# Causal mask of the transposed scores by selection on GpSimd, K stacks on ScalarE's queue, gap rows written by SyncE

## What is computed

```python
h = _layernorm(x) * (1 + ca) + sa
q = h @ w_dq.T @ w_uq.T ; kv = h @ w_dkv.T @ w_ukv.T ; k, v = split(kv)
attn = einsum('bhqd,bhkd->bhqk', q, k) * SCALE + triu(-inf, k=1)   # causal
x = x + ga * (softmax(attn) @ v) @ w_out.T
h = _layernorm(x) * (1 + cb) + sb
top = argmax(softmax(h @ Wg.T))              # expert 0 (gelu) or 1 (relu)
x = x + gb * where(top == 0, expert0(h), expert1(h))
```

## Time and profile before

| What | Value |
|---|---|
| runs before, median (lowest, highest) | 584.45 us (584.08, 586.81) |
| profiled execution, whole | 587.29 us |
| its span | 585.5 us |
| PE / DVE / ACT / POOL busy | 80% / 74% / 50% / 39% |
| granted clock of TensorE, mean | 0.901 |

### The profile page before, as it was taken

One profiled execution on the slowest core, in us unless ns is written; L12 is line 12 of the kernel. 1 busy time (PEld: TensorE's weight loads), 2 busy tenths in 40 slices (PEclk: granted clock), 3 DMA queues, 4 the chain that ended last, 5 costly groups with the idle time before them and its releaser, 6 DMA issues. The chain is left out here.

```text
span 585.5 us, 11643 instructions
## 1 busy us (share of the span) xinstructions
PE 466.7 (80%) x4137; PEld 368.5 (63%) x4137; DVE 432.9 (74%) x988; ACT 293.1 (50%) x425; POOL 227.6 (39%) x245
## 2 busy tenths in 40 slices
PE   4634799998978989989989889857705999999950
PEld 4323577776766867767767677634504988888840
DVE  3666576998879878978988798742651699989970
ACT  1342366754635547547447356414402777766630
POOL 8422122334414334334344234273240045455565
PEclk9958799998989889989989899976955999999995
DMA  8578459768748678788688497384339604460111
GB/s 259 181 105 113 80 100 145 99 127 177 101 137 184 103 159 162 129 165 159 127 171 120 110 190 121 98 314 158 119 127 343 231 19 158 150 213 4 37 54 54
DMA packets 58696, 82.02 MB, mean 140 GB/s; under 512 B 7039, under 2 KB 47104, under 8 KB 58640
## 3 DMA queue, kind: packets, MB, share of 16 engines
q1 hardware_dynamic: 52576, 59.37, 48.8%
q0 software_dynamic: 5248, 21.53, 10.9%
q10 hardware_dynamic: 816, 0.39, 0.3%
HBM read 34.12 MB, written 22.11 MB: 96 GB/s over the span
## 5 line engine op out<-in xcount | busy, mean ns | idle before, releaser
L1109 DVE TENSOR_REDUCE mx<-ps_s 128x2 f32<-128x512 f32 (+1 forms) x192 | 124.2, 685 | 49.6 <-PE ps_s L436 47.9
L860 ACT ACTIVATE p_all<-ps_t 128x1024 f32<-128x1024 f32 x93 | 95.3, 1024 | 119.3 <-PE ps_t L436 107.9
L456 PE MATMUL ps_s<-ks,qs 96*128 96x256 bf16 (+1 forms) x512 | 73.6, 253 | 41.1 <-issue 32.8
L456 PEld LDWEIGHTS ps_s<-ks,qs 96*128 96x128 bf16 x512 | 39.6, 100 | 57.5 <-issue 47.2
L482 PE MATMUL ps_t<-qs,ks 99*128 99x128 bf16 (+1 forms) x496 | 61.0, 258 | 6.8 <-DMA qs<-mx_rows 3.1
L436 PE MATMUL ps_s<-future_b,ident_b 128*128 128x256 bf16 (+1 forms) x192 | 62.4, 325 | 0.0
L1360 POOL TENSOR_TENSOR comb<-z,xs 128x512 f32<-128x512 f32 x16 | 20.6, 1285 | 98.3 <-DVE z L1172 98.3
L482 PEld LDWEIGHTS ps_t<-qs,ks 99*128 99x128 bf16 x496 | 38.8, 101 | 21.8 <-issue 12.3
L1467 POOL TENSOR_TENSOR tile_rows<-tile_rows 128x512 f32<-128x512 f32 x18 | 26.3, 1464 | 62.6 <-DVE tile_rows L1292 62.5
L1348 POOL TENSOR_TENSOR ln_rs<-ln_ve,neg_half 128x2 f32<-128x2 f32 x32 | 22.7, 710 | 64.8 <-DVE ln_ve L960 63.7
L403 PE MATMUL ps_s<-down_w,hid_hi 128*128 128x256 f32 x144 | 41.5, 288 | 4.9 <-DVE hid_lo L1272 4.9
(11 more groups left out here) (210 smaller groups left out, 1251.7 us busy)
## 6 DMA issues: line engine op xcount, KB each, us to landing
qs<-parts_q SPq DMA_DIRECT2D x96, 128.0 KB
ks<-parts_k SPq DMA_DIRECT2D x96, 128.0 KB
tile_rows<-sorted_scratch SPq DMA_DIRECT2D x9, 1026.0 KB, 11.7
rows<-mod_rows_scratch SPq DMA_DIRECT2D x16, 384.0 KB, 4.7
tile_rows<-sorted_scratch SPq DMA_DIRECT2D x9, 512.0 KB, 5.3
xs<-x SPq DMA_DIRECT2D x16, 256.0 KB, 5.0
comb<-mod_rows_scratch SPq DMA_DIRECT2D x32, 128.0 KB, 4.4
p_all<-wmod SPq DMA_DIRECT2D x1, 1024.0 KB, 5.9
```

The source lines that it names most:

```text
L456: pe.matmul(ps_s[:, n * width:(n + 1) * width], qs[b.third][0:R, h, tile * P:(tile + 1) * P], ks[b.third][0:R, h, 0:width], start=n % a_ba ...
L860: act.activation((p0, p1)[tile][:, h0:h0 + n, :], scores_t(b, c)[:].rearrange("p (h s) -> p h s", h=n), ACT.Exp, scale=SCALE).then_inc(exp ...
L1109: dve.tensor_reduce(mx[:, tile, h0:h0 + n], ps_s[:, 512 * bank:512 * (bank + 1)].rearrange("p (h k) -> p h k", h=n), AX_X, ALU.max).then_i ...
```

## The change

- The two `past_b` matmuls of every transposed chunk go. In their place `hide_future` on POOL replaces, in `p0` and `p1` after the exponential, what lies above the diagonal by zero, with one `affine_select` per chunk (96 in all: 64 of 128 x 512 elements, 32 of 128 x 1024). `values` waits for `exp_masked` instead of `exp_done`.
- `stack_k` of parts 0 and 1 (five DMAs a batch) moves from SyncE's queue to ScalarE's; part 2 stays on SyncE's. On ACT `k_second` moves ahead of `exponentials(at(3), 0)`; on DVE `k_rest` moves ahead of `place`; on POOL `k_third` and `number_rows` move ahead and `put_rows` moves to the end of the step.
- `fill_gap` with its 12 indirect DMAs goes. After the last batch SyncE reads the gap's first row from `gap_slot` (a copy of `n_first`) and writes exactly 512 rows from `wa` by two plain DMAs, columns 0 to 255 ahead of `load_g(0)`, the others behind it. `load_rest` waits for the second; `load_g` runs three tiles ahead instead of one.
- The set-up on POOL loses one memset, one select and one copy.

```diff
@@ SyncE
                 stack_q(at(1), 0)
                 stack_q(at(1), 1)
-                stack_k(at(1), 0)
                 stack_q(at(1), 2)
-                stack_k(at(1), 1)
-                stack_k(at(1), 2)
+                stack_k3(at(1))
...
+            sp.wait_ge(gap_slot_ready, 1)
+            gap_rows = sorted_dram[bass.ds(sp.value_load(gap_slot[0:1, 0:1], min_val=0, max_val=TOKENS), TS), :].rearrange("(j p) w -> p j w", p=P)
+            some = wa[0][:].rearrange("p k f -> p (k f)").bitcast(F32)
+            sp.dma_start(gap_rows[:, :, 0:D], some[:, 0:D].unsqueeze(1).to_broadcast([P, TJ, D])).then_inc(g_filled, 16)
             for n in range(2):
                 sp.wait_ge(put[n], 16 * NB)
+            sp.wait_ge(g_filled, 16)
             load_g(0)
+            sp.dma_start(gap_rows[:, :, D:ROW], some[:, D:ROW].unsqueeze(1).to_broadcast([P, TJ, ROW - D])).then_inc(rest_filled, 16)
+            load_g(1)
+            load_g(2)
+            sp.wait_ge(rest_filled, 16)
             for i in range(NT):
-                load_g(i + 1)
                 load_rest(i)
+                load_g(i + 3)
@@ TensorE, st_chunk and values
-                for bank in range(2):
-                    mm = masked(dst[:, bank * 512:(bank + 1) * 512], a_bank, 0, past_b)
                 mm.then_inc(st_done, 1)
...
-                pe.wait_ge(exp_done, CH * b.n + ST_OF_GROUP[g])
+                pe.wait_ge(exp_masked, CH * b.n + ST_OF_GROUP[g])
@@ ScalarE
+            def stack_k(b, part):
+                if b.off:
+                    return
+                wait(act, st_done, CH * (b.n - 2))
+                wait_alone(act)
+                act.wait_ge((k1_ready, k2_ready)[part], b.n + 1)
+                for n in range(NSPLIT):
+                    if SPLITS[n][1] == part:
+                        act.dma_start(ks[b.third][n * HD:(n + 1) * HD, :, :], parts_k[:, part, :]).then_inc(k_in[b.pair], 16)
...
                 values_copy(at(4), 1)
+                stack_k(at(1), 0)
+                k_second(at(1))
                 exponentials(at(3), 0)
+                stack_k(at(1), 1)
                 v_copy(at(1))
-                k_second(at(1))
                 exponentials(at(3), 1)
@@ GpSimd
+            def hide_future(b, c):
+                if b.off:
+                    return
+                pool.wait_ge(exp_done, CH * b.n + c + 1)
+                tile, h0, n = ST[c]
+                diag = (p0, p1)[tile][:, h0:h0 + n, 0:P]
+                pool.affine_select(out=diag, in_=diag, compare_op=ALU.is_ge, fill=0.0, base=0,
+                                   pattern=[[0, n], [1, P]], channel_multiplier=-1).then_inc(exp_masked, 1)
```

More of the change, by code:

```diff
@@ L116, in block_kernel @@
         row_of = [sb(f"row_of{i}", [P, TJ], I32) for i in range(2)]
[L117 to L120, removed]
+        gap_slot = sb("gap_slot", [P, 1], I32)
         attention = ctx.enter_context(ExitStack())
@@ L181, in block_kernel @@
         cT_raw, c_silu = mx[:], mx_rest[:]
-        past, future, below = (flat[0][:, 4 * D + i * P:4 * D + (i + 1) * P] for i in range(3))
+        future, below = (flat[0][:, 4 * D + i * P:4 * D + (i + 1) * P] for i in range(2))
         mod_rows = flat[1][0:NB, 0:4 * D].rearrange("p (r d) -> p r d", d=D)
@@ L211, in block_kernel @@
         s_done, max_done, max_split, mt_done = (sem(n) for n in "s_done max_done max_split mt_done".split())
-        mt_ready, st_done, exp_done, pv_done, o_ready = (sem(n) for n in "mt_ready st_done exp_done pv_done o_ready".split())
+        mt_ready, st_done, exp_done, exp_masked, pv_done, o_ready = (sem(n) for n in
+            "mt_ready st_done exp_done exp_masked pv_done o_ready".split())
         ot_done, rden_ready, attn_ready, at_done, a_hi_ready, a_lo_ready, op_done, gated_ready, x1_ready = (sem(n) for n in
@@ L247, in block_kernel @@
         LAGS = 6
-        CONSTS = 13
+        CONSTS = 10
         TABLES = 7
@@ L324, in stack_q, with stack_k3 @@
                 stack(b, part, 0, parts_q, qs, (q1_ready, q2_ready, q3_ready), q_in)
-            def stack_k(b, part):
-                stack(b, part, 1, parts_k, ks, (k1_ready, k2_ready, k3_ready), k_in)
+            def stack_k3(b):
+                stack(b, 2, 1, parts_k, ks, (k1_ready, k2_ready, k3_ready), k_in)
             load_x(Batch(0, NB))
@@ L481, in st_chunk @@
                 for h in range(n):
-                    pe.matmul(dst[:, h * width:(h + 1) * width], ks[b.third][0:RM, h0 + h, tile * P:(tile + 1) * P],
-                              qs[b.third][0:RM, h0 + h, tile * P:S], start=h % a_bank == 0, stop=False)
-                for bank in range(2):
-                    mm = masked(dst[:, bank * 512:(bank + 1) * 512], a_bank, 0, past_b)
+                    mm = pe.matmul(dst[:, h * width:(h + 1) * width], ks[b.third][0:RM, h0 + h, tile * P:(tile + 1) * P],
+                              qs[b.third][0:RM, h0 + h, tile * P:S], start=h % a_bank == 0, stop=h % a_bank == a_bank - 1)
                 mm.then_inc(st_done, 1)
@@ L1198, in step @@
                 row_max(at(2), 2)
+                k_rest(at(1))
                 place(at(6))
[L1200 removed]
                 second_stats(at(5))
@@ L1220, in _ @@
             dve.wait_ge(total_ready, 1)
+            dve.tensor_copy(gap_slot[:], n_first[:]).then_inc(gap_slot_ready, 1)
+            dve.wait_ge(tables_made, TABLES)
             dve.tensor_scalar(tile_second[:], tile_start[:], n_first[:], None, ALU.is_ge).then_inc(bits_ready, 1)
@@ L1447, in step @@
             def step(at):
+                hide_future(at(4), 4)
                 add_attn(at(5))
                 later_inverse(at(0))
+                hide_future(at(4), 5)
                 q_third(at(1))
+                hide_future(at(3), 0)
+                k_third(at(1))
                 inverse_deviation(at(5), 1)
+                hide_future(at(3), 1)
+                number_rows(at(5))
+                hide_future(at(3), 2)
+                h_low(at(0))
+                hide_future(at(3), 3)
                 put_rows(at(6))
[L1453 to L1456, removed]
             pipeline(step)
```

29 lines of the change are left out of this document (5 added, 24 removed).

## The result

The changed kernel takes 602.22 us (median of four runs, 599.56 to 607.72) where the kernel before, beside it, takes 584.50: 1.031 times as long, 95% interval 1.022 to 1.039. The forecast was 560 us. The ratios further down are each taken against runs of the kernel before made beside that experiment, whose medians lie between 582.2 and 584.3; so times of different experiments compare to some 2 us.

What follows compares the result with a forecast made beforehand. The stack loop with puts among the stacks was taken as the bound. Eleven steps -17.8, early step +1.5, fill -11, tail +1, seam +1.5: -24.8, from 587.29 to 562.5 profiled, or 584.45 to 560 us; range 542 to 580.

Steps and rivals of the forecast that it cites:

- What bounds the kernel before: Steady attention steps: scores, projection, twelve stacks with another batch's puts among them, next scores; 22.72 us a step, 19.64 without puts.
- slower, through the puts: Steady steps: `add_attn` waits for puts just issued, with selects and inverse deviation queued behind; about 609 us, chance 0.09.
- 13.2 + L: Puts' loop: landing L, then add, DVE to `a_hi`, exponentials, copy, select, put issues; 16.5 us at L 3.3, binding from 8.
- The sign that I had named for it: On POOL, `add_attn` would wait over 4 us for a DMA, with `values` waiting behind it.
- Eleven steps: Steady attention steps with puts, 119.97 to 369.87 us: 21.1 us each for 22.72, -17.8 in all.
- ScalarE's issues: Five K issues on ACT cost 3.15 us a step, 1.62 hidden under ACTIVATEs; the remaining 1.53 lengthens the second loop.
- Selects on POOL: Between exponentials and `values`: 0.75 us short, 1.4 long, counted 0 in steady steps; extra slowing of DVE also 0.
- the second loop: Steady steps, through DVE and ACT from `row_max` to the next: 19.56 us without waits for PE, 21.1 after the change.
- Early steps: Attention steps before any puts: only the one of 19.64 us counted, going to 21.1, +1.5.
- The fill: Twelve indirect gap DMAs on POOL starve the engines at the pipeline's end; removing them gives -11 us, between 8 and 14.
- Tail: Last four attention steps: selects ahead of `values` add about 0.8 each where masks saved 0.3; +1 us, 0 to 3.
- Seam: Between last put and first feed-forward load: gap columns must land too; +1.5 us, 0 to 4.

Runs made afterwards that it cites:

- `add_attn` late: Changed kernel with `add_attn` moved on POOL behind the select of chunk (4,5) and the first inverse deviation: 580.64 us, 1.001 times the kernel before.
- the buffers in place: 64 unused bytes put `qs`, `ks` and the parts on multiples of 256 bytes: changed kernel 603.95 us; with `add_attn` late as well, 578.58 us.
- the fastest kernel: Changed kernel with `add_attn` late, 64 unused bytes aligning the stacks' buffers, mask back on TensorE and all stacks on SyncE: 558.76 us, 0.959 times the kernel before.
- both kernels shifted: Stacks' buffers off multiples of 256 bytes: kernel before with 192 unused bytes ahead of them, 607.71 us, against the gap-only kernel, 596.27 us.
- the gap-only kernel: Kernel before with only `fill_gap` replaced by SyncE's two DMAs and the later `load_g`: 596.27 us; with 64 unused bytes aligning the stacks' buffers, 576.34 us.

## Why the prediction was wrong

**What bounds the kernel before:** right. The stack loop was the bound, and with the puts last PE's wait before `s_chunk` went. But what then took its place was not weighed rightly. One reading behind it was wrong without harm: the 1.11 of the earlier trace rows is not the twelve stacks' alone, since the puts' queue has part in that window. SyncE's queue holds 88.5% there and the puts' 22.4%; but from 245 to 247.4, ahead of the puts, SyncE's alone holds 112.4%.

**The step that failed** is the last rival, "slower, through the puts", to which I gave 0.09 as 13.2 + L, binding from L = 8. Its path was wrong. I followed the rest through DVE to `a_hi`, while what stands directly behind `add_attn` on POOL, the inverse deviation and the select that PE wants, leads on through `values`, the copy of `oT`, the issues on ACT and two exponentials. In the terms of that sum, where L counts from the end of the second issue and both issues are in the rest, the round of 25.0 is 18.6 + 6.4. So the loop passes 21.1 from L = 2.5 and not from 8. L was also read too low: 3.3 at the earlier trace rows, where the queue was idle, and 4.8 to 6.5 in the nine landings that stand in the chain of the eleven steps (6.0 to 7.6 from the start of the second issue). But L alone would not have done it, 13.2 + 6.4 = 19.6 stays below 21.1; the missing 5.4 us of the rest are the error. I had written down what queues behind the wait and then not followed it to its end. That this rival's 25.2 us a step and 609 us, at L = 12, lie so near the round of 25.0 and the 602 measured is luck: an L assumed too long stood beside a rest too short. The sign that I had named for it came true: `add_attn` waits up to 5.9 us for a DMA, and `values` behind it.

**Eleven steps:** -17.8 forecast, +9.4 measured. With `add_attn` late it is -7.7 (242.17), and with the buffers in place -11.4. **ScalarE's issues:** the overlap that was assumed is there, issues begin under a running ACTIVATE (306.06 under the copy that began at 306.00 and took 0.60):

```profile
306.00 0.60 ACT L765 ACTIVATE oT<-ps_o 128x512 f32<-128x512 f32 x1 [2.85 <-PE ps_o L504]
306.06 1.91 ACTq L822 DMA_DIRECT2D ks<-parts_k  x3
308.02 0.63 ACT L811 ACTIVATE parts_k<-rest_k 128x512 bf16<-128x512 f32 x1 [1.42 <-DVE rest_k L1157]
308.56 1.01 ACT L875 ACTIVATE p_all<-ps_t 128x1024 f32<-128x1024 f32 x1
308.68 1.20 ACTq L822 DMA_DIRECT2D ks<-parts_k  x2
```

The next ACTIVATE begins at 308.02, after the third issue has ended. The term of 1.53 a step was too large: 0.2 to 0.5 in the eleven steps with the late `add_attn`, 0.8 where the puts' loop binds (23.6 for 22.8). The row also shows what I had not seen: the stacks of K's first part, which was written by 303.15, wait until the copy ahead of them may start.

**Selects on POOL:** 0.75 and 1.4 assumed, 0.64 and 1.17 in the mean measured, near enough. That POOL's new list slows DVE by 0 was wrong: DVE's busy time is 20.6 a step with the selects and 19.5 with the mask on TensorE (ScalarE's stacks in both), and the second loop closed in 21.7, not 21.1. How much of it is the selects' own is open: with SyncE's stacks the same pair is 20.4 and 20.2, since in the fastest kernel, without a select, `z<-xs` still takes 696 ns, beside `add_attn` and the third part of Q. **Early steps:** +1.5 forecast, +5.6 measured, of which 3.2 are the place of the buffers (82.5 against 85.7). The forecast gave a term to one of the four steps only; 21.1 in each of them would have been 84.4 for 80.1, +4.3.

**The fill:** -11 forecast, -13.7 and, both kernels shifted, -14.2 (67.5 to 53.4) measured; the size was a little low. **Tail:** +1 forecast. With the mask on PE it would be about nothing, with selects it is +6 to +9; so the stage came out at -3.0 (62.6) and not at -10, of which 3.6 are still the puts' loop (59.0 with the late `add_attn`). This is the second failed term, by its size. **The sum:** eleven steps 27.2 us over the forecast, early steps 4.1, fill and tail 7.0, all else 1.2 below it, together the 37.1 between 562.5 and the profiled execution's 599.56. **Seam:** +1.5 forecast, +1.3 measured: the last put ends at 448.57, and the rows answering to the earlier trace rows are

```profile
447.61 0.96 POOL L1392 DMA_INDIRECT sorted_scratch<-comb,pos  x1 [0.30 <-issue]
447.96 0.41 SPq L390 DMA_DIRECT2D sorted_scratch<-wa  x1
452.85 0.39 SPq L379 DMA_DIRECT2D tile_rows<-sorted_scratch  x1
```

**What had no term at all:** the place of the stacks' buffers. It did not cause the miss, since the changed kernel takes 604 us with them in place, and with the late `add_attn` it is worth 2 us, or up to 6, as another loop binds. But where the stacks bind it costs 10 to 24 us: 24 and 23 in the kernel before, 20 in the gap-only kernel, 10 in the fastest.

## What to carry to other kernels

When a slow transfer is issued late in an in-order engine's list and awaited near the front of the next round, follow every instruction queued behind it to the end of its chain, and take the transfer's time from a busy stretch, not from an idle seam (4.8 to 6.5 us against 3.3 here). A stage that changes although none of its instructions did (263.5 us for 249.9 here, by 192 unused bytes) can be a sign that an address has moved: compare the starts of the buffers before looking for a cause in the order. Count the latency of work given to a less busy engine in the last batches too: the selects on POOL cost at most 3.2 us in the eleven full steps and 6.1 to 9.4 in the stage behind them.

## What was unexpected of the hardware

- In the early steps, packets of 1024 bytes, most of them of SBUF to SBUF copies, took 105 ns from and to buffers that start on a multiple of 256 bytes, and 116 and 118 ns from and to ones 64 and 192 bytes past it; the kernel before went from 584 to 608 us by that.
- An `affine_select` on POOL took 0.64 us for 128 x 512 and 1.09 to 1.36 for 128 x 1024 elements in the changed kernel.
- DVE's `z<-xs` of 128 x 256 took 401 to 411 ns alone, 0.72 us beside a select, 1.24 beside the third part of Q on POOL (both in the changed kernel) and up to 1.50 beside `add_attn`, and `z<-comb` 0.48 alone and 0.86 beside a select. DVE was busy for 19.4 us a step in the kernel before and 20.6 with the late `add_attn` and the buffers in place.
- An indirect put of 128 rows of 3076 bytes landed 6.0 to 7.6 us after the start of its issue within a step.
